# Second attention: how a chunk's two half results leave the bank, and which engine adds up the rows of head 1

## The reference

```
Q_std, K_std, V = heads(...); Q_low, K_low = heads(...)      # 16 heads, head size 32
scores = einsum('bhtd,bhsd->bhts', Qf, Kf) / sqrt(32)
scores = where(causal, scores, min)
attn   = softmax(scores, axis=-1)
out    = einsum('bhts,bhsd->bhtd', attn, V)
y      = out.transpose(0, 2, 1, 3).reshape(B, T, C);  return y @ Wp
```

## Time and profile before

| | |
|---|---|
| median of 3 runs | 2858.85 us (2844.64 to 2863.61) |
| the profiled execution | 2851.66 us, span 2849.9 us |
| TensorE clock granted, mean | 0.887 of full speed |
| second attention in the span | from about 2053 to 2755 us, steps from 2054.3 us |
| busy in the span | PE 2509.2, DVE 1733.5, ACT 1219.1, POOL 525.8 us |

### The profile page before, as it was taken

The page is one execution under the profiler, slowest core; times in us unless marked ns, Lnnn a source line. Parts: engine busy times, 40 slices in busy tenths (PEclk is TensorE's granted clock), DMA queues, the critical chain, the costliest instruction groups (busy, mean ns, idle before and its releaser), DMA issues. The chain is left out here.

```text
span 2849.9 us, 38069 instructions
## 1 busy us (share of the span) xinstructions
PE 2509.2 (88%) x14418; PEld 1586.2 (56%) x14418; DVE 1733.5 (61%) x2023; ACT 1219.1 (43%) x2325; POOL 525.8 (18%) x479
## 2 busy tenths in 40 slices
PE   4959999779999999999995899879698989999856
PEld 2748888545555545555542577768444444544415
DVE  3644544376876878778731543322488888877843
ACT  2422222116776777767662222122054444544431
POOL 1210000100000000000000012200165656655550
PEclk8979999857997999999975999989599989988878
DMA  4761100242212112120002200055622221120014
GB/s 136 224 199 45 45 29 15 24 57 35 33 22 41 30 27 40 23 36 9 9 6 85 90 20 1 0 126 192 138 47 61 60 59 32 36 61 8 9 56 141
DMA packets 121375, 164.43 MB, mean 58 GB/s; under 512 B 60848, under 2 KB 66608, under 8 KB 115824
## 3 DMA queue, kind: packets, MB, share of 16 engines
q1 hardware_dynamic: 117744, 149.52, 21.7%
q10 hardware_dynamic: 3456, 12.58, 1.4%
HBM read 114.19 MB, written 47.71 MB: 57 GB/s over the span
## 5 line engine op out<-in xcount | busy, mean ns | idle before, releaser
L705 DVE TENSOR_REDUCE a_mx_part<-a_ps 128x2 f32<-128x1024 f32 (+3 forms) x640 | 652.9, 1060 | 205.4 <-PE a_ps L627 101.6
L600 ACT ACTIVATE a_ex<-a_ps_s 128x512 f32<-128x512 f32 (+3 forms) x1280 | 603.7, 538 | 361.2 <-PE a_ps_s L653 202.6
L648 PE MATMUL a_ps_s<-a_q,a_k 50*128 50x512 f32 (+3 forms) x1280 | 493.7, 458 | 4.0 <-ACT a_ex L600 3.8
L973 ACT ACTIVATE a_ex<-a_ps_s 128x512 f32<-128x512 f32 (+3 forms) x640 | 319.8, 533 | 400.9 <-PE a_ps_s L1030 205.8
L619 PE MATMUL a_ps<-a_k,a_q 48*128 48x512 f32 (+3 forms) x1280 | 425.2, 465 | 49.9 <-DMA a_q<-q 29.1
L948 POOL TENSOR_TENSOR a_acc<-a_acc,a_ex 128x512 f32<-128x512 f32 (+1 forms) x336 | 389.9, 1160 | 203.3 <-ACT a_ex L973 179.6
L648 PEld LDWEIGHTS a_ps_s<-a_q,a_k 50*128 50x128 f32 x1280 | 234.2, 203 | 307.6 <-ACT a_ex L600 227.0
L1091 DVE TENSOR_REDUCE a_mx_part<-a_ps 128x2 f32<-128x1024 f32 (+2 forms) x320 | 335.3, 1054 | 84.5 <-PE a_ps L994 52.0
L667 PE MATMUL a_ps_o<-a_ex,a_v 128*32 128x512 f32 (+3 forms) x2560 | 338.1, 604 | 0.0
L994 PE MATMUL a_ps<-a_k,a_q 96*128 96x512 f32 (+3 forms) x640 | 234.1, 435 | 38.3 <-DMA a_q<-q 23.4
L1610 POOL TENSOR_TENSOR gc_z<-gc_state,gc_qg 128x512 f32<-128x512 f32 x16 | 26.3, 1641 | 1242.3 <-DVE gc_qg L1598 1242.3
(11 more groups left out here) (192 smaller groups left out, 3755.9 us busy)
## 6 DMA issues: line engine op xcount, KB each, us to landing
a_q<-q SPq DMA_DIRECT2D x48, 256.0 KB, 5.4
a_k<-k SPq DMA_DIRECT2D x24, 512.0 KB, 4.9
a_q<-q SPq DMA_DIRECT2D x24, 512.0 KB, 6.9
q<-p_oh SPq DMA_DIRECT2D x32, 256.0 KB, 2.5
q<-p_ol SPq DMA_DIRECT2D x32, 256.0 KB, 2.8
w_o<-o SPq DMA_DIRECT2D x8, 1024.0 KB
w_z<-z SPq DMA_DIRECT2D x32, 256.0 KB
a_k<-k SPq DMA_DIRECT2D x48, 128.0 KB, 3.4
```

The lines of the kernel that those rows point to most:

```text
L600: act.activation(ex[unit % NE][:, h % 2, off:CH], ps_s[n % 3][:, off:CH], ACT.Exp, scale=SCALE)\
L648: mm = pe.matmul(ps_s[n % 3][:, off:CH], k_st[st][r0:r0 + KM, h % KH, t * P:(t + 1) * P], q_st[st][r0:r0 + KM, slot_h, c * CH + off:(c + 1 ...
L705: dve.tensor_reduce(mx_part[:, 2 * p:2 * p + 2, i, kc], bank[:, :, 0:w], AX.X, ALU.max).then_inc(taken1, 1)
L973: act.activation(ex[s % NE][:, h, off:CH], ps_s[n % 3][:, off:CH], ACT.Exp, scale=SCALE)\
```

## The change

ACT now copies both halves of `ps_o`, the even one (partitions 0 to 63, always 512 columns) to a new tile `o_even` after its first exponential of step L+3, and the odd one to `o_odd` after its second exponential of that step (`take_o`). PE's product waits for these two copies (`taken_o`) and no longer for `staged`. POOL adds the two tiles into `o_sb` (`join`) ahead of its add of step L+4; for the last chunk it does so after its last add. DVE's join is gone. The third accumulator and its product are gone: POOL adds head 0 in every step and waits only for the exponential of head 0; DVE adds head 1 in every step.

```diff
--- before.py
+++ after.py
@@ -787,16 +787,6 @@
 
         return range(0, LEAD1) if s < 0 else range(s + LEAD1, s + LEAD1 + 1)
 
-    def pool_adds(s):
-
-        g, c, t = STEP_LIST[s]
-        return c > 0 and t % TPC == TPC - 1
-
-    def adds_through(s, pool):
-
-        n = sum(pool_adds(x) for x in range(s + 1))
-        return s + 1 + n if pool else s + 1 - n
-
     with ExitStack() as ctx:
         def sb(n, shape, dt=F32):
             return ctx.enter_context(nc.sbuf_tensor(f"{name}_{n}", shape, dt))
@@ -811,9 +801,9 @@
         k_st = [sb(f"k{i}", [P, HG, TOK], F32R) for i in range(NS)]
         v_st = [sb(f"v{i}", [P, HG, QT, DH]) for i in range(NS)]
         ex = [sb(f"ex{i}", [P, HG, CH]) for i in range(NE)]
-        acc = [[sb(f"acc{i}_{n}", [P, CH]) for n in range(3)] for i in range(2)]
+        acc = [[sb(f"acc{i}_{n}", [P, CH]) for n in range(HG)] for i in range(2)]
         one = sb("one", [P, DH])
-        o_odd = [sb(f"o_odd{i}", [OR, CH]) for i in range(2)]
+        o_even, o_odd = [[sb(f"o_{n}{i}", [OR, CH]) for i in range(2)] for n in ("even", "odd")]
         o_sb = [sb(f"o{i}", [OR, CH]) for i in range(2)]
         z_sb = [sb(f"z_sb{i}", [OR, CH]) for i in range(2)]
         mx_part = sb("mx_part", [P, HG, QT, NCH])
@@ -833,7 +823,7 @@
         rows_in = [sem(f"rows_in{i}") for i in range(2)]
         scores2, exp_done, pv_done = sem("scores2"), sem("exp_done"), sem("pv_done")
         added0, added1 = sem("added0"), sem("added1")
-        odd_out, staged = sem("odd_out"), sem("staged")
+        taken_o, staged = sem("taken_o"), sem("staged")
         stored = [sem(f"stored{i}") for i in range(2)]
         z_stored = [sem(f"z_stored{i}") for i in range(2)]
         z_in = [sem(f"z_in{i}") for i in range(NZ)]
@@ -931,48 +921,62 @@
         def _(pool):
             for s in range(NS):
                 pool.memset(k_st[s][KC:P].bitcast(F32), 1.0).then_inc(blank, 1)
-            done = 0
+            def join(g, c):
+
+                j = g * NCH + c
+                c0 = P if c == 0 else 0
+                pool.wait_ge(taken_o, 2 * (j + 1))
+                if j >= 2:
+                    pool.wait_ge(stored[j % 2], 16 * (j // 2))
+                if c0 > 0:
+                    pool.tensor_copy(o_sb[j % 2][:, 0:c0], o_even[j % 2][:, 0:c0])
+                pool.tensor_tensor(o_sb[j % 2][:, c0:CH], o_even[j % 2][:, c0:CH], o_odd[j % 2][:, c0:CH], ALU.add)\
+                    .then_inc(staged, 1)
+
+            pool.wait_ge(blank, NS)
             for s, (g, c, t) in enumerate(STEP_LIST):
-                j, off, tile = g * NCH + c, first_col(c, t), ex[s % NE]
-                pool.wait_ge(exp_done, (s + 1) * HG)
-                if t == 0 and j >= 2:
-                    pool.wait_ge(scores1, SUMS_ENTRY[j - 2] + 1)
-                for h, total in ((0, acc[j % 2][0]), (1, acc[j % 2][2]))[0:1 + pool_adds(s)]:
-                    if done > 0:
-                        pool.wait_ge(added0, done)
-                    else:
-                        pool.wait_ge(blank, NS)
-                    if t == 0 or (h, t) == (1, TPC - 1):
-                        pool.tensor_copy(total[:, :], tile[:, h, :]).then_inc(added0, 1)
-                    else:
-                        pool.tensor_tensor(total[:, off:CH], total[:, off:CH], tile[:, h, off:CH], ALU.add).then_inc(added0, 1)
-                    done += 1
+                if s - 4 in LAST_STEP:
+                    join(*LAST_STEP[s - 4])
+                j, off = g * NCH + c, first_col(c, t)
+                total, tile = acc[j % 2][0], ex[s % NE][:, 0, off:CH]
+                pool.wait_ge(exp_done, s * HG + 1)
+                if t == 0:
+                    if j >= 2:
+                        pool.wait_ge(scores1, SUMS_ENTRY[j - 2] + 1)
+                    pool.tensor_copy(total[:, :], tile).then_inc(added0, 1)
+                else:
+                    pool.wait_ge(added0, s)
+                    pool.tensor_tensor(total[:, off:CH], total[:, off:CH], tile, ALU.add).then_inc(added0, 1)
+            join(GROUPS - 1, NCH - 1)
 
         @block.scalar
         def _(act):
-            def odd_part(g, c, d):
+            def take_o(g, c, d, odd):
 
                 j = g * NCH + c
-                c0 = P if c == 0 else 0
-                act.wait_ge(pv_done, d + 1)
-                if j >= 2:
-                    act.wait_ge(staged, j - 1)
-                act.activation(o_odd[j % 2][:, c0:CH], ps_o[OR:P, c0:CH], ACT.Copy).then_inc(odd_out, 1)
+                c0 = P if c == 0 and odd else 0
+                if not odd:
+                    act.wait_ge(pv_done, d + 1)
+                    if j >= 2:
+                        act.wait_ge(staged, j - 1)
+                part, tile = (ps_o[OR:P, c0:CH], o_odd[j % 2]) if odd else (ps_o[0:OR, :], o_even[j % 2])
+                act.activation(tile[:, c0:CH], part, ACT.Copy).then_inc(taken_o, 1)
 
             for s, (g, c, t) in enumerate(STEP_LIST):
-                if s - 4 in LAST_STEP:
-                    odd_part(*LAST_STEP[s - 4], (s - 4) // 2)
                 off = first_col(c, t)
                 for h in range(HG):
                     n = s * HG + h
                     act.wait_ge(scores2, n + 1)
                     if h == 0 and s >= NE:
                         act.wait_ge(pv_done, (s - NE) // 2 + 1)
-                        act.wait_ge(added0, adds_through(s - NE, True))
-                        act.wait_ge(added1, adds_through(s - NE, False))
+                        act.wait_ge(added0, s - NE + 1)
+                        act.wait_ge(added1, s - NE + 1)
                     act.activation(ex[s % NE][:, h, off:CH], ps_s[n % 3][:, off:CH], ACT.Exp, scale=SCALE)\
                         .then_inc(exp_done, 1)
-            odd_part(GROUPS - 1, NCH - 1, len(STEP_LIST) // 2 - 1)
+                    if s - 3 in LAST_STEP:
+                        take_o(*LAST_STEP[s - 3], (s - 3) // 2, h)
+            for odd in range(2):
+                take_o(GROUPS - 1, NCH - 1, len(STEP_LIST) // 2 - 1, odd)
 
         @block.tensor
         def _(pe):
@@ -1008,15 +1012,13 @@
             def sums(n):
 
                 j, m = SUMS_AT[n], sums_entry(n)
-                s, c = n - LEAD1 - Z_AFTER, j % NCH
+                s = n - LEAD1 - Z_AFTER
                 pe.wait_ge(taken1, m - 1)
-                pe.wait_ge(added0, adds_through(s, True))
-                pe.wait_ge(added1, adds_through(s, False))
-                bank = ps_1[m % 2]
-                pe.matmul(bank[0:DH, 0, :], one[:, :], acc[j % 2][0][:, :], start=True, stop=True)
-                mm = pe.matmul(bank[DH:OR, 0, :], one[:, :], acc[j % 2][1][:, :], start=True, stop=c == 0)
-                if c > 0:
-                    mm = pe.matmul(bank[DH:OR, 0, :], one[:, :], acc[j % 2][2][:, :], start=False, stop=True)
+                pe.wait_ge(added0, s + 1)
+                pe.wait_ge(added1, s + 1)
+                for h in range(HG):
+                    mm = pe.matmul(ps_1[m % 2][h * DH:(h + 1) * DH, 0, :], one[:, :], acc[j % 2][h][:, :],
+                                   start=True, stop=True)
                 mm.then_inc(scores1, 1)
 
             def scores(s, h):
@@ -1040,7 +1042,7 @@
                     pe.wait_ge(v_landed[g % NS], 16 * (g // NS + 1))
                 pe.wait_ge(exp_done, (2 * d + 2) * HG)
                 if t0 == 0 and g * NCH + c > 0:
-                    pe.wait_ge(staged, g * NCH + c)
+                    pe.wait_ge(taken_o, 2 * (g * NCH + c))
                 last = t0 == TPC * c + TPC - 2
                 for odd in range(2):
                     t, s = t0 + odd, 2 * d + odd
@@ -1122,28 +1124,14 @@
                 g, c, t = STEP_LIST[s]
                 j, off = g * NCH + c, first_col(c, t)
                 total, tile = acc[j % 2][1], ex[s % NE][:, 1, off:CH]
-                if pool_adds(s):
-                    return
                 dve.wait_ge(exp_done, (s + 1) * HG)
                 if t == 0 and j >= 2:
                     dve.wait_ge(scores1, SUMS_ENTRY[j - 2] + 1)
                 if t == 0:
                     dve.tensor_copy(total[:, :], tile).then_inc(added1, 1)
                     return
-                dve.wait_ge(added1, adds_through(s - 1, False))
+                dve.wait_ge(added1, s)
                 dve.tensor_tensor(total[:, off:CH], total[:, off:CH], tile, ALU.add).then_inc(added1, 1)
-
-            def join(g, c):
-
-                j = g * NCH + c
-                c0 = P if c == 0 else 0
-                dve.wait_ge(odd_out, j + 1)
-                if j >= 2:
-                    dve.wait_ge(stored[j % 2], 16 * (j // 2))
-                if c0 > 0:
-                    dve.tensor_copy(o_sb[j % 2][:, 0:c0], ps_o[0:OR, 0:c0])
-                dve.tensor_tensor(o_sb[j % 2][:, c0:CH], ps_o[0:OR, c0:CH], o_odd[j % 2][:, c0:CH], ALU.add)\
-                    .then_inc(staged, 1)
 
             def invert(g, c):
 
@@ -1154,8 +1142,6 @@
```

(2 more changed lines are left out.)

## The result

The changed kernel takes 2755.23 us (median of 4 runs, 2737.13 to 2768.20) against 2861.23 us before (4 runs): a ratio of 0.963, 95% interval 0.9571 to 0.9689, some 106 us faster. The profiled execution of the changed kernel is 2768.20 us, its slowest: its first exponential of the stage falls at 2070.7 us, before the change at 2054.3 us, after the same code. The stage itself is what to compare.

The account below looks back on a forecast made before the run. DVE was taken to bound c = 3, and PE's waits for DVE's join plus the slow clock behind them to cost time elsewhere; chunk terms summed to 55.7 us off 2851.66, 2796, set at 2803 beside the median, range 2768 to 2845 us.

Parts of the forecast that it names:

- Part 4: POOL: nine adds a group leave, four joins of 1.26 us arrive; POOL stays off the path, effect taken as 0.
- Part 1: PE's wait for the bank: without DVE's join PE starts 1.00 us sooner and keeps 0.67 us of waiting.
- Part 3: DVE takes nine more adds a group, each full add 0.38 us over its bare length; c = 3 becomes 32.4 us.
- Part 2: The row sums' third product goes 24 times: worth 1.7 us in c = 2, 0.9 elsewhere, nothing where DVE limits.
- (b): Without the 1.67 us gap PE's clock stays at its upper level in all chunks: 77 us gained, 2782 us; chance 0.20.
- (a): DVE also limits c = 1 and c = 2, bank waits become waits for the maxima: 20 us gained, 2838 us; chance 0.14.
- (c): In c = 3 PE starves behind DVE and the clock falls twice each time: 33 us slower, 2892 us; chance 0.09.
- (d): Bank release no earlier, odd copy hanging on an exponential that PE's scores hold back: 6 us, 2853 us; chance 0.09.

Follow-up runs that it names:

- late wait: GpSimd's add waits for the exponentials of both heads, as in the kernel before; put back alone into the changed kernel: 2812.35 us, ratio 0.9863 to the kernel before.
- E: GpSimd's add of head 0 waits for head 0's exponential only, not both heads'; alone against the kernel before: 2789.13 us, ratio 0.9764.
- S: Row sums: VectorE adds head 1 in every step, no third accumulator or product; alone against the kernel before: 2844.01 us, ratio 0.9965.
- R: Release of the bank: ScalarE copies both halves out, GpSimd joins them; alone against the kernel before: 2792.36 us, ratio 0.9778.
- R and S: Bank release and row sums together: with the late wait 2812.35 us, ratio 0.9863 to the kernel before; with E it is the changed kernel, 2755.23 us.

## Why the prediction was wrong

Stage lengths in us, each from one profile, put the three parts side by side; in brackets the time in the stage at a granted clock of 0.50, added up from the trace:

| | late wait | with E |
|---|---|---|
| neither | 689.7 (143) | 620.8 (43) |
| S | 695.8 (190) | 615.2 (62) |
| R | 623.9 (45) | 602.4 (36) |
| R and S | 647.3 (77) | 593.4 (40) |

R alone and E alone each take away some 100 us at the lower clock, and they largely take away the same 100 us: that is much of why 66 and 69 us do not add up, but give 87 us together. If the lower clock cost half of its time, it was up to 50 us of either gain; this is an estimate, and an upper bound. S is the part that depends on E: on top of R it costs 23 us with the late wait and gains 9 us with E.

- **The step that failed** is one that I never took: the diff's `pool.wait_ge(exp_done, s * HG + 1)` has no price in Part 4, which took POOL as off the path. It is worth 69 us alone and 54 us on top of the rest, as much as the release. POOL was off the path, but its adds share turns with DVE's, and their moment decides how long DVE waits and, where the join stands behind DVE's copy, how long TensorE does. The change without E measured 2812 us, within 10 us of the 2803 us forecast: in the total I had priced that kernel, though not chunk by chunk (its mean c = 1 is 18.3 us and not 16.8, its full c = 3 30.9 us and not 32.4).
- **Part 1, the release**, is right in kind: 66 us alone, but only 22 us on top of S and E. The forecast of 0.67 us left per wait came out at 0.50 us. The clock behind the gap came back in c = 2 in all groups, and in c = 3 in all but the last; I had counted on part of it (23.0 us for c = 2; 21.6 us measured).
- **Part 3, DVE's work**, sized the wait of an add by today's mean, 0.38 us; measured 0.21 us in the same chunk, 0.25 us in the other full groups. My 32.4 us for c = 3 is wrong for the change (28.5 us). That S alone gave 31.9 to 33.4 us is in part luck, since the clock had fallen there, and without E the change has c = 3 at 30.6 us in five of the seven full groups. That term alone is 7 x 3.9 = 27 us of the missing 48 (2803 less 2755); c = 2 is 7 x 1.4 = 10 us more, and the rest is spread over c = 0, c = 1 and what lies outside the stage.
- **Part 2, the third product**, was 21 us or more in the sum; put back at full clock it costs 0.8 us in each c = 1 and c = 2 and nothing in c = 3, 7.9 us net. It may have been worth more before, where in c = 2 it ran at half clock; no run takes it out alone.
- **Part 4, POOL**: the join took 1.28 us, as the 128-partition add had, so partitions do not count. The version with the join on DVE takes 39 us of such joins off POOL over the stage (406.5 against 367.4 us busy).
- **Of the rivals**, (b) was nearest, at 2782 us, for its clock; it too had c = 3 at 31.4 us. In (a), DVE's need of 16.3 and 22.0 us in c = 1 and c = 2 was close (15.5 and 21.5 us), but taken with the old waits. (c) needed waits of 1 us; they fell instead. (d) is excluded by the wait for ACT's copy.

The Trainium skill, SBUF — State Buffer, "Who interferes with whom", also says that issue order decides who blocks. The trace agrees: VectorE's copy took 1.12 us when it started 0.43 us behind a GpSimd add, and 0.64 us at the same place with E, where GpSimd's add was nearly over. The same instructions, with GpSimd's start moved by half a step, made 647.3 or 593.4 us of stage. What I had taken from that page was only that the moved adds must wait. I had also given its exemption for at most one SBUF input without the page's condition, that VectorE is outside its two-port modes. VectorE's copy has one such input and did wait.

What stays open: why a step late suits c = 3 and not c = 2. The two engines fall into an order that depends on the widths and on the stall before, and no run here isolates it. Nor was the idle time behind which the clock falls swept. In the c = 2 moments shown it fell behind 1.67 us and behind 0.62 and 0.96 us in a row, and did not behind 1.16 or 0.49 us. But before the change it also stayed up behind 2.13 us in four of the c = 1 chunks and behind 1.47 us in five of the c = 3 chunks, so the length of one wait does not decide it.

## What to carry to other kernels

When two engines take turns at a resource, price the moment at which each asks and not only the work, and read a diff for its waits as closely as for its instructions. Change the waits alone, one by one, before work is moved: here one number in one wait, alone, gave two thirds of what a change of four engines gave (2.4 of 3.7%). An engine that is busy to within a quarter of a microsecond of a whole chunk may be filled by its own waits; take a piece of work off it before you call it the limit.

## What the hardware showed that I had not expected

- A GpSimd add of 64x512 takes as long as one of 128x512: 1.28 and 1.26 us.
- A VectorE instruction that waits for its turn shows as a longer instruction and not as idle time: the same 128x512 add is 0.68 us alone and was 1.58 us behind a GpSimd add, and the 128x512 copy took 0.47 us in one place and 1.12 us in the other.
- A gap of 1.67 us in a TensorE that is otherwise busy was followed by 6.83 us at half clock, and with a gap of 0.49 us the clock stayed at 1.00 through all c = 2 and c = 3 chunks but the last, where the gap was 1.17 us. In c = 0 and c = 1 it still fell in some groups.
